# A Flamingo block on one core: scores of a pair of batches as one float32 product of 128 by 128 by 128 in place of two of rounded parts, queries and keys kept unsplit

## What is computed

```python
q = (layernorm(x) @ Wq).reshape(b, 64, 32, 128)      # 32 batches
k = (ctx @ Wk).reshape(b, 64, 32, 128)
v = (ctx @ Wv).reshape(b, 64, 32, 128)
score = einsum('bqhd,bkhd->bhqk', q, k) / sqrt(128) + position_bias
probs = softmax(where(mask, score, -inf))            # zero where masked
x = x + tanh(g_xattn) * (einsum('bhqk,bkhd->bqhd', probs, v).reshape(b, 64, 4096) @ Wo)
y = layernorm(x) @ weight.T + bias + lora(layernorm(x))
x = x + tanh(g_ffn) * y
```

## Time and profile before

| | |
|---|---|
| median of 3 runs | 1724.48 us (1724.07 to 1725.8) |
| the profiled execution | 1723.98 us, of which its span 1722.2 us |
| TensorE busy (PE) | 1702.7 us, 99% of the span, 8535 matmuls |
| weight loads busy (PEld) | 1438.4 us, 84%, 8535 loads |
| VectorE busy (DVE) | 1226.4 us, 71% |
| ScalarE busy (ACT) | 691.9 us, 40% |
| GpSimd busy (POOL) | 900.5 us, 52% |
| granted clock of TensorE | 0.999 of the full one |

### The profile page before, as it was taken

The page is one execution under the profiler, slowest core; times in us unless marked ns, Lnnn a source line. Parts: engine busy times, 40 slices in busy tenths (PEclk is TensorE's granted clock), DMA queues, the critical chain, the costliest instruction groups (busy, mean ns, idle before and its releaser), DMA issues.

```text
span 1722.2 us, 25763 instructions
## 1 busy us (share of the span) xinstructions
PE 1702.7 (99%) x8535; PEld 1438.4 (84%) x8535; DVE 1226.4 (71%) x2648; ACT 691.9 (40%) x1473; POOL 900.5 (52%) x1187
## 2 busy tenths in 40 slices
PE   8999999999999999999999999999999999999998
PEld 7888888888888888888888888888888888888886
DVE  5777667777676665666777777577777777777775
ACT  5555555554334442444333433233333333333331
POOL 5767767765466654555455644454534444343431
PEclk9999999999999999999999999999999999999999
DMA  7777777766667764757777876586766667667541
GB/s 277 278 261 264 270 271 277 275 245 217 219 232 247 254 227 165 257 202 246 251 245 279 279 275 235 172 320 240 268 222 246 222 223 248 223 218 244 197 143 44
DMA packets 162856, 407.95 MB, mean 237 GB/s; under 512 B 15554, under 2 KB 56642, under 8 KB 162724
## 3 DMA queue, kind: packets, MB, share of 16 engines
q1 hardware_dynamic: 162580, 406.05, 67.4%
q10 hardware_dynamic: 144, 0.26, 0.0%
HBM read 313.97 MB, written 92.27 MB: 236 GB/s over the span
## 4 chain that ended last, share of the span: by engine, by line
PE 89%; DVE 5%; issue 2%; POOL 2%; ACT 1%; DMA 1%; SPq 0%; DVEq 0%; ACTq 0%; POOLq 0%
PE vo_bank L397 12%; PE vo_bank L399 11%; PE vo_bank L398 11%; PE q_bank L397 7%; PE q_bank L399 7%; PE q_bank L398 7%; PE k_bank L397 6%; PE k_bank L399 6%; PE k_bank L398 6%; PE s_two L402 5%; PE pv_two L402 5%; PE s_two L403 2%; PE pv_two L403 2%; DVE score L1241 1%; DVE pv_two L1221 1%
## 5 line engine op out<-in xcount | busy, mean ns | idle before, releaser
L1523 POOL TENSOR_TENSOR score<-score,row_max 128x256 f32<-128x256 f32 x128 | 78.6, 614 | 553.5 <-DVE row_max L1246 553.5
L1434 POOL TENSOR_TENSOR ot_lo<-attn,ot_hi 128x512 fp32r<-128x512 f32 x128 | 165.7, 1294 | 174.8 <-ACT ot_hi L936 174.8
L1032 ACT ACTIVATE attn<-pv_two 128x512 f32<-128x512 f32 x128 | 76.5, 597 | 373.4 <-PE pv_two L403 373.3
L397 PE MATMUL q_bank<-xt_hi,wq 128*128 128x512 f32 x512 | 208.1, 406 | 0.0
L399 PE MATMUL q_bank<-xt_hi,wq 128*128 128x512 f32 x512 | 200.4, 391 | 0.0
L398 PE MATMUL q_bank<-xt_lo,wq 128*128 128x512 f32 x512 | 200.0, 391 | 0.0
L397 PE MATMUL k_bank<-ct_hi,wk 128*128 128x512 f32 x512 | 199.3, 389 | 0.6 <-DVE ct_lo L1159 0.6
L398 PE MATMUL k_bank<-ct_lo,wk 128*128 128x512 f32 x512 | 199.2, 389 | 0.0
L399 PE MATMUL k_bank<-ct_hi,wk 128*128 128x512 f32 x512 | 199.2, 389 | 0.0
L397 PE MATMUL vo_bank<-wo,ot_hi 128*128 128x512 f32 x496 | 193.1, 389 | 1.0 <-POOL ot_lo L1434 1.0
L399 PE MATMUL vo_bank<-wo,ot_lo 128*128 128x512 f32 x496 | 193.0, 389 | 0.0
(11 more groups left out here) (220 smaller groups left out, 4206.5 us busy)
## 6 DMA issues: line engine op xcount, KB each, us to landing
wq<-wq_split SPq DMA_DIRECT2D x96, 512.0 KB, 3.3
wk<-wk_split SPq DMA_DIRECT2D x96, 512.0 KB, 3.7
wo<-wo_split SPq DMA_DIRECT2D x96, 512.0 KB, 5.5
wv<-wv_mixed SPq DMA_DIRECT2D x32, 1024.0 KB, 7.7
wv<-wv_split SPq DMA_DIRECT2D x24, 1024.0 KB, 6.5
raw_bias<-in_pair_bias SPq DMA_DIRECT2D x64, 256.0 KB, 5.7
wq_split<-wq SPq DMA_DIRECT2D x32, 512.0 KB, 2.9
wk_split<-wk SPq DMA_DIRECT2D x32, 512.0 KB, 4.2
```

Of the source, the lines that this page charges most:

```text
L397: pe.matmul(to, left[0], right[0], start=first, stop=False)
L1434: pool.tensor_tensor(to, src, f32(of), ALU.subtract).then_inc(done, 1)
```

## The change

The queries `qt` and the keys `kt` become plain float32 tiles without a second part. ScalarE copies the two banks into them as before (now signalling `q_out` and `k_out`); VectorE's two subtractions per slot are gone. TensorE's waits on `q_lo` and `k_lo` become waits on `q_out` and `k_out`. The scores are one float32 matmul of 128 columns for each tile m instead of the two of `both`; the second half of `s_two` is not written by them. VectorE's scores are one pass instead of two, and `score_done` takes the place of `score_b_done` for the bias load. The attention product is as it was.

```diff
-        qt = two("qt", [P, BLK])
-        kt = sb("kt", [P, PB, 2, P], F32R)
+        qt = sb("qt", [P, BLK], F32)
+        kt = sb("kt", [P, PB, P], F32)
...
-                wait(sp, score_b_done, 2 * m - 2)
+                wait(sp, score_done, 2 * m - 2)
...
-                wait(pe, q_lo, n)
+                wait(pe, q_out, n)
...
-                wait(pe, k_lo, n)
+                wait(pe, k_out, n)
...
                 if job in IN_QUERY_BANK:
-                    pe.wait_ge(q_lo, n + 1)
+                    pe.wait_ge(q_out, n + 1)
...
-                pe.wait_ge(q_lo, n + 1)
-                pe.wait_ge(k_lo, n + 1)
+                pe.wait_ge(q_out, n + 1)
+                pe.wait_ge(k_out, n + 1)
+                wait(pe, score_done, n)
                 for m in range(PB):
-                    mm = both(pe, s_two[:, m, :, :], parts(qt, slice(None), cols(m, P)), kt[:, m, :, :])
+                    mm = pe.matmul(s_two[:, m, 0, :], qt[:, cols(m, P)], kt[:, m, :], start=True, stop=True)
                 mm.then_inc(s_ps, 1)
...
-                hi(qt[0][:, :], q_bank[:, :], q_hi)
+                hi(qt[:, :], q_bank[:, :], q_out)
...
-                hi(k_part(0), by(k_bank, PB), k_hi)
+                hi(kt[:, :, :], by(k_bank, PB), k_out)
...
-            def queries(n):
-                dve.wait_ge(q_hi, n + 1)
-                lo(qt[1][:, :], q_bank[:, :], qt[0][:, :], q_lo)
-
-            def keys(n):
-                dve.wait_ge(k_hi, n + 1)
-                lo(k_part(1), by(k_bank, PB), k_part(0), k_lo)
...
-                for part, plus, done in ((1, raw_bias[m % 2][:, n % 2, :, :], score_b_done),
-                                         (0, score[:, :, :], score_done)):
-                    for a in range(2):
-                        rows = cols(a, S)
-                        last = dve.scalar_tensor_tensor(out=score[rows, :, :], in0=s_two[rows, :, part, rows],
-                                                        scalar=SCALE, in1=plus[rows, :, :],
-                                                        op0=ALU.mult, op1=ALU.add)
-                    last.then_inc(done, 1)
-                    dve.wait_ge(done, n + 1)
+                for a in range(2):
+                    rows = cols(a, S)
+                    last = dve.scalar_tensor_tensor(out=score[rows, :, :], in0=s_two[rows, :, 0, rows],
+                                                    scalar=SCALE, in1=raw_bias[m % 2][rows, n % 2, :, :],
+                                                    op0=ALU.mult, op1=ALU.add)
+                last.then_inc(score_done, 1)
+                dve.wait_ge(score_done, n + 1)
                 dve.tensor_reduce(row_max[:, :], score[:, :, :], X, ALU.max).then_inc(max_done, 1)
```

More of the change, by code:

```diff
@@ L341, in flamingo_block @@
         q_ps, k_ps, s_ps, pv_ps, vo_ps = (sem(f"{m}_ps") for m in ("q", "k", "s", "pv", "vo"))
[L342 to L345, removed]
+        q_out, k_out = sem("q_out"), sem("k_out")
+        turn_hi, v_hi, pt_hi, ot_hi, wq_hi, wk_hi, wv_hi, wo_hi, stage_hi, lead_ct_hi, lora_hi = (
+            sem(f"{m}_hi") for m in ("turn", "v", "pt", "ot", "wq", "wk", "wv", "wo", "stage", "lead_ct", "lora"))
+        v_lo, pt_lo, ot_lo, wq_lo, wk_lo, wv_lo, wo_lo, stage_lo, lead_ct_lo, lora_lo = (
+            sem(f"{m}_lo") for m in ("v", "pt", "ot", "wq", "wk", "wv", "wo", "stage", "lead_ct", "lora"))
         wq_saved, wk_saved, wv_saved, wo_saved, wq_back, wk_back, wv_back, wo_back = (
@@ L350, in flamingo_block @@
             sem(f"{m}_done") for m in ("gate", "exp", "var", "pow", "bias"))
-        score_b_done, score_done, max_done, shift_done, sum_done, inv_done, rscale_done, prob_done = (
-            sem(f"{m}_done") for m in ("score_b", "score", "max", "shift", "sum", "inv", "rscale", "prob"))
+        score_done, max_done, shift_done, sum_done, inv_done, rscale_done, prob_done = (
+            sem(f"{m}_done") for m in ("score", "max", "shift", "sum", "inv", "rscale", "prob"))
         product_in, sums_in, weights_in = ([sem(f"{m}_in{i}") for i in range(2)] for m in ("product", "sums", "weights"))
@@ L391, in halves @@
             return t[:, 0:HALF], t[:, HALF:2 * HALF]
-        def k_part(part):
-            return kt[:, :, part, :]
         def mm3(pe, to, left, right, first, last):
@@ L1339, in slot @@
                 if n > 0:
-                    queries(n)
                     if n >= G:
@@ L1343, in slot @@
                     transposes(n - 1)
-                    keys(n)
                     rest_of_probabilities(n - 1)
@@ L1391, in _ @@
                 turn(LEAD, 0, t)
-            keys(0)
             dve.wait_ge(mask_in, 16)
             dve.tensor_reduce(row_kept[:, :], mask_u8[:, :, :], X, ALU.max).then_inc(kept_done, 1)
-            queries(0)
             dve.wait_ge(kept_done, 1)
```

## The result

The changed kernel takes 1708.87 us (median of 4, 1708.38 to 1709.46), the kernel before 1724.33 beside it: a ratio of 0.9908, 95% interval 0.9896 to 0.992. That is 15.5 us saved where 7.7 were forecast. The time lies inside the range, and the sign was right, but the size was off by a factor of two.

A forecast was written before the change was run, and what follows sets the result against it. The prediction took TensorE's distance between starts and its few waits to bound the kernel: 1724.5 + 2.6 (scores and attention stream) − 10.3 (waits) = 1716.8, say 1717 us. The range, 8 times in 10, was 1706 to 1750.

The forecast's parts named there:

- The form of a float32 product: Scores on TensorE: each tile's unsplit product makes two loads and two passages of 256 columns.
- rivals 1: Scores on TensorE: a gap stays between the two halves of a float32 product; 1742 or 1775 us, chance 0.12.
- rival 2: Scores on TensorE: each of the four part products has a load of its own; 1836 us, chance 0.14.
- The price of a passage: Scores on TensorE: 0.119 us per 256-column passage, scores 0.08 us longer a slot; by the transpositions 0.11 each.
- The swap of 0.06 us at the attention's first load: Attention on TensorE: its first load fits under the last score passage, so 0.87 us instead of 0.93 a slot.
- VectorE's relief: VectorE loses 285 us of work; TensorE's waits on it shrink, 10.3 us saved in all.
- the scores' 2.1 us: TensorE's scores waited 3.0 us for the keys' rest; with ScalarE's copy enough, 2.1 us is saved.
- the additions: TensorE's transpositions waited 4.1 us for VectorE's additions, behind both rests; 4.0 us saved.
- the adapter's 1.0: The adapter products on TensorE waited 1.0 us behind VectorE's additions; all of it goes.
- GpSimd's: The outputs on TensorE waited 2.6 us for GpSimd's rest of the attention; 1.0 us saved.
- 14 times 0.16: TensorE's waits cost more than their rows show: 14 waits at 0.16 us each, 2.2 us more saved.
- Rival 3: TensorE's waits stay, on the previous product, normalisation or GpSimd's own queue; 1726 us, chance 0.10.

The follow-up runs named there:

- doubling: The changed kernel with every float32 product of the scores made twice into the same place: 1822.2 us.
- the relieved kernel: Changed kernel, but TensorE makes the old score pairs with rests that are zeros written once; VectorE's rests and second score pass stay gone: 1710.7 us, ratio 0.9928.
- the product alone: Changed kernel's float32 scores, with VectorE's two subtractions, a second score pass (scale 0) and the old waits kept: 1725.8 us against 1723.9 for the kernel before.

## Why the prediction was half right

**The form of a float32 product** was right: two loads, two passages of doubled columns, and nothing of rivals 1 (from 1742) and 2 (1836). Four passes through the array, as the Trainium skill states in "FP8 and Floating Point Precision", section "TensorE Precision Notes", agree with a 275 ns duration at 128 columns in each of two rows; that each pass brings a load of its own, as rival 2 had it, is refuted by 1024 loads for 512 products.

**The price of a passage** is the first step that failed. I had 0.119 from ordinary matmuls of 256 columns and 0.11 from the float32 transpositions, and chose the first. Measured by doubling, it is 0.111. Over 1024 passages the difference is some 8 us of the sum. Both halves of it were float32 streamed twice, and so was the row that I put aside; the row of the same operands would have been the nearer one.

**The swap of 0.06 us at the attention's first load** came only in part. The load does start with the last score passage (807.70), but the attention is drawn 0.95 us long and not 0.87, and the first query matmul takes 0.30 us until the next (808.68 to 808.98), where it took 0.28. With the transposition's price and the swap the prediction had −6.4 for the stream; measured by starts, on top of the relief, it is −3.3, and by the times −1.4 to −3.4. The sum had +2.6.

**VectorE's relief** is the second step that failed, in what it was made of more than in its size. The sum had 10.3 us; alone it is 12.4 (10 to 15). Of the single terms the scores' 2.1 us held (3.0 to 0.9); the additions gave 2.4 and not 4.0 in the changed kernel, the adapter's 1.0 nothing, GpSimd's 1.8 and not 1.0. The additions' waits were put down to the two rests ahead of them in their slot, and it was chiefly the second score pass: with the rests back the wait is 1.3 us, with the pass back 4.3. The shown waits fell by 5.4 us in all (15.1 to 9.7, the sums of the view), less than the 8.1 forecast and under the 6 below which the prediction called itself wrong (TensorE's idle time, span less busy, fell by 6.2, from 19.5 to 13.3). What lay beside the shown waits was more than my 14 times 0.16, or 2.2: TensorE's busy time fell by 7.1 us in the relieved kernel, with the same matmuls. The other sign, a score group over 1.01 us, did not come; it takes 0.81. Next time the distances between starts are to be summed over the whole trace, not sampled at one place.

**Rival 3**, that the waits stay, is refuted by the relieved kernel; a weaker form of it, that saved stream time goes into waits, is just what the product alone shows: 3.3 us more lost in waits by the count of starts, and no gain in time.

The sum of my two terms was −7.7 and the measured one −15.5. With the relief first, some 4 to 6 us of the difference are the stream's and 2 to 3 the relief's; the starts in the traces say the same (−3.3 against +2.6). The split depends on the order, though: the product added first costs 1.8 us (0 to 3 by the interval), close to my +2.6, but by luck, since there the stream's gain went into waits, and the relief on top of it then gives 16.9 where I had 10.3.

## What to carry to other kernels

Where an engine at 99% waits for one at 71%, the second engine's work has no fixed price: here one and the same pass of 0.86 us a slot cost 7.6, 15.8 or 52 us depending on what else stood in its row. Find out by putting single pieces of work back which of them the waits hang on; here it was the pass ahead of the softmax, while the two rests, longer together, cost 1.1 us without it. Don't expect a faster stream on the first engine to show before the second one has room. In these groups of short matmuls, each with a load of its own, the number of loads fits the cost and the columns don't, so one product of unsplit float32 (two loads, twice the columns each) costs no more than one of rounded parts and saves all the splitting.

## What was not expected of the hardware

A float32 product of 128 columns with loads of its own costs 0.221 us in a row of such, one of 64 moving columns the same to within 1%, and the pair of rounded parts (256 and 128 columns) 0.229 by the starts and 0.235 by the time, though it streams a quarter fewer columns than the 512 of the other. The loads of the pairs come at unequal distances: from the load of a pair's 256-column matmul to that of its 128-column one it is 0.11 us, from there to the next pair's 0.12 (medians 0.109 and 0.121 in the kernel before). Why the second is longer no run here shows.
